# Second mixture of a twelve-stage decoder: its weighted sum on TensorE by diagonals, and earlier first work in two mixtures and a cross-attention

## What is computed

```python
# L2 cross-attention: 16 heads of 64, no softmax
q, k, v = split(layernorm(Q) @ wq), split(layernorm(K) @ wk), split(layernorm(V) @ wv)
out = (l2norm(q) @ l2norm(k).T) @ v            # computed as l2norm(q) @ (l2norm(k).T @ v)
x = Q + out @ wo + bo;  return x + gelu(layernorm(x) @ w1 + b1) @ w2 + b2

# L2 mixture: 8 experts, two per token, each takes at most C = 538 rows
gates = softmax(xf @ Wg.T);  topw, topi = top_k(gates, 2)
within = place_in_expert < C
y = gelu(rows @ W1[e] + b1[e]) @ W2[e] + b2[e]
x = x + sum(topw[:, r] * within[:, r] * y[row of (token, r)] for r in (0, 1))
```

## Time and profile before

| | |
|---|---|
| median of 3 runs | 2631.78 us (2630.09 to 2638.85) |
| the profiled execution | 2638.47 us, span 2637.1 us |
| PE busy, share of the span | 2356.0 us, 89% |
| DVE, ACT, POOL busy | 1207.8, 924.0, 573.2 us |
| mean granted clock of PE | 0.942 of 2.4 GHz |

### The profile page before, as it was taken

One profiled execution on the slowest core, in us unless ns is written; L12 is line 12 of the kernel. 1 busy time (PEld: TensorE's weight loads), 2 busy tenths in 40 slices (PEclk: granted clock), 3 DMA queues, 4 the chain that ended last, 5 costly groups with the idle time before them and its releaser, 6 DMA issues. The chain is left out here.

```text
span 2637.1 us, 34511 instructions
## 1 busy us (share of the span) xinstructions
PE 2356.0 (89%) x13630; PEld 1598.1 (61%) x13630; DVE 1207.8 (46%) x2321; ACT 924.0 (35%) x2500; POOL 573.2 (22%) x587
## 2 busy tenths in 40 slices
PE   6885999998998999786899999689995899989999
PEld 5674777767675665223466656668883478744555
DVE  5644222255787473656234431410006566677442
ACT  2211222242674461554232232022222456434331
POOL 1621222232001011201354420033312100043110
PEclk9977999999999899898899999789997999989999
DMA  5015888840001000200000000322315833210000
GB/s 167 0 33 219 302 303 301 301 157 1 1 2 53 1 2 32 100 1 32 0 1 1 0 1 0 112 73 93 98 45 202 327 148 139 81 36 1 9 9 17
DMA packets 75383, 224.29 MB, mean 85 GB/s; under 512 B 9359, under 2 KB 52757, under 8 KB 65238
## 3 DMA queue, kind: packets, MB, share of 16 engines
q1 hardware_dynamic: 67894, 204.82, 21.4%
q0 software_dynamic: 7328, 17.26, 1.9%
HBM read 178.68 MB, written 45.17 MB: 85 GB/s over the span
## 5 line engine op out<-in xcount | busy, mean ns | idle before, releaser
L221 PE MATMUL psum<-arena 128*128 128x256 f32 (+4 forms) x3716 | 987.5, 423 | 16.1 <-ACT arena L231 3.9
L221 PEld LDWEIGHTS psum<-arena 128*128 128x128 f32 (+1 forms) x3716 | 681.3, 186 | 279.8 <-issue 130.1
L263 POOL TENSOR_SCALAR x_moments<-x_moments 128x4 f32<-128x4 f32 x48 | 12.5, 260 | 879.9 <-DVE x_moments L256 879.5
L1964 DVE TENSOR_REDUCE small<-psum 128x4 f32<-128x1024 f32 (+1 forms) x112 | 137.0, 1223 | 116.4 <-PE psum L1875 65.6
L1234 POOL DMA_INDIRECT l_out<-arena,slot_tables x79 | 78.6, 996 | 412.4 <-ACT arena L1412 234.0
L1937 ACT ACTIVATE arena<-psum,small 128x128 f32<-128x128 f32 (+1 forms) x384 | 148.8, 414 | 51.5 <-DVE small L1964 51.3
L3555 PE MATMUL psum<-arena 128*128 128x512 bf16 x768 | 166.2, 379 | 0.0
L1439 DVE TENSOR_TENSOR arena<-arena,psum 128x352 f32<-128x352 f32 x78 | 40.6, 521 | 253.7 <-ACT arena L1390 253.7
L1975 DVE COPY arena<-psum 128x512 f32<-128x512 f32 x224 | 143.5, 680 | 1.7 <-PE psum L1886 1.5
L1870 PE MATMUL psum<-arena 32*128 32x128 f32 (+1 forms) x1280 | 133.1, 339 | 0.0
L1937 ACT ACTIVATE z<-psum,small 128x128 f32<-128x128 f32 (+1 forms) x256 | 103.8, 426 | 74.8 <-DVE small L1964 74.8
(11 more groups left out here) (360 smaller groups left out, 3480.9 us busy)
## 6 DMA issues: line engine op xcount, KB each, us to landing
arena<-L_ffn_w_in SPq DMA_DIRECT2D x39, 2176.0 KB
arena<-L_ffn_W_in SPq DMA_DIRECT2D x16, 1024.0 KB
positions<-arena SPq DMA_DIRECT2D x16, 1024.0 KB, 5.2
arena<-positions SPq DMA_DIRECT2D x16, 1024.0 KB, 7.8
arena<-l_out SPq DMA_DIRECT2D x16, 512.0 KB, 7.7
positions<-arena SPq DMA_DIRECT2D x16, 512.0 KB, 5.2
arena<-positions SPq DMA_DIRECT2D x16, 512.0 KB, 8.5
arena<-ctx_in SPq DMA_DIRECT2D x2, 2048.0 KB, 10.3
```

What stands on the lines that cost most here:

```text
L221: last = nc.tensor.matmul(out, lhsT, rhs, start=(n == 0), stop=(n == len(pairs) - 1))
L1964: nc.vector.reduce_max(self.minus_top(h), use.bank(u).rearrange("p (h l) -> p h l", l=L), AX_X, negate=True).then_inc(self.topped.up(), 1)
```

## The change

**The second mixture's end.** ACT writes 32 diagonal matrices (the identity scaled by the weight of a choice) behind its last strip. For each group PE waits for both ranks, multiplies each returned tile of rows by the diagonal of its weights and adds the pair in PSUM (8 products of 128 x 256), in banks 0 and 1, 2 and 3, 4 and 5, 0 and 1; DVE adds the bank pair to x in one instruction of 128 x 1024. The next norm's transposes stand between the sums on PE.

```diff
+    def pe_sum(self, g):
+        nc, use, u = self.k.nc, self.uses, self.sum_use[g]
+        bank = use.take(u)
+        for rank in range(2):
+            self.k.pe.wait_ge(self.fetched[g][rank])
+        for j in range(4):
+            i = 4 * g + j
+            mm = products(nc, bank[:, D * j:D * j + D], [(self.diagonals[:, rank, i, :], self.back[:, rank, i, :])
+                                                         for rank in range(2)])
+        mm.then_inc(use.fills(u), 1)
+    def act_diagonals(self):
+        k, act = self.k, self.k.act
+        act.wait_ge(self.router.weighed)
+        act.wait_ge(*self.uses.filled(self.y_use[E - 2][-1]))
+        for rank in range(2):
+            for i in range(TILES):
+                m = k.nc.scalar.activation(self.diagonals[:, rank, i, :], k.ident, ACT.Copy,
+                                           scale=self.router.weights[:, rank, i:i + 1])
+        m.then_inc(self.diagonals_in.up(), 1)
+    def dve_sum(self):
+        k, use = self.k, self.uses
+        for g, u in enumerate(self.sum_use):
+            xs = k.x[:, 4 * g:4 * g + 4, :]
+            k.dve.wait_ge(*use.filled(u))
+            k.nc.vector.tensor_tensor(xs, xs, use.bank(u).rearrange("p (a c) -> p a c", a=4),
+                                      ALU.add).then_inc(use.empties(u), 1)
+            self.next.norm.dve_final(g, use.emptied(u))
...
-        self.finals("pe")
+        pe.wait_ge(self.diagonals_in)
+        for g in range(GROUPS):
+            self.pe_sum(g)
+            self.next.norm.pe_final(g)
...
-        self.dve_combine()
+        self.dve_sum()
```

```diff
+    def pe_turn_first(self, part):
+        use, tiles = self.uses, (range(self.FIRST), range(self.FIRST, self.RT))[part]
+        for a in tiles:
+            self.k.pe.wait_ge(self.first_rows[a])
+        for c in range(DC):
+            u = self.turn_use[0][2 * part + c]
+            self.turned(0, use.take(u), c, tiles).then_inc(use.fills(u), 1)
...
-        self.pe_turn(0)
+        self.pe_turn_first(0)
...
                 for m, u in enumerate(self.h_use[e][half]):
+                    if (e, half, m) == (0, 0, MT // 2):
+                        self.pe_turn_first(1)
```

```diff
+        if self.capacity is not None:
+            dve.wait_ge(self.chosen)
+            dve.step(nc.vector.tensor_tensor(place3, hot3, k.count_up[:, 0:E].unsqueeze(1).to_broadcast([P, 32, E]), ALU.mult))
+            dve.step(nc.vector.reduce_sum(base, place3, AX_X))
         dve.wait_ge(*use.filled(self.use_counts))
...
-        for n, part in enumerate(k.choice_parts):
-            nc.vector.tensor_tensor(self.parts[:, :, tiles * n:tiles * n + tiles], high,
-                                    part.unsqueeze(2).to_broadcast([P, N, tiles]), ALU.mult)
+        nc.vector.tensor_tensor(self.parts[:, :, 0:tiles], high, k.choice_parts[0].unsqueeze(2).to_broadcast([P, N, tiles]),
+                                ALU.mult)
...
     def act(self):
         self.norm.act_zT(GROUPS - 1)
+        self.k.act.wait_ge(self.tiles_in)
+        self.k.nc.scalar.activation(self.parts[:, :, self.tiles:2 * self.tiles], self.tile_hot, ACT.Copy,
+                                    scale=self.k.choice_parts[1][:, 0:1]).then_inc(self.places_in.up(), 1)
```

```diff
+        self.q_use.extend(u.add("sums", 2) for _ in range(2))
+        for g in range(GROUPS):
+            self.ctx_turn.use.append([u.add(engine, 1, 4 + 2 * (g % 2) + c) for c, engine in enumerate(("dve", "act"))])
         context()
-        queries()
...
+        self.norm.pe_zT(0)
+        for mark in self.norm.zT_in(0):
+            pe.wait_ge(*mark)
+        self.pe_queries(0)
         for g in range(GROUPS):
             self.ctx_turn.pe(g, (self.ctx_normed, 4 * g + 4))
...
         self.pe_context(0)
-        self.pe_queries(0)
...
+        self.dve_queries(0)
         self.dve_context(0)
-        self.dve_queries(0)
```

More of the change, by code:

```diff
@@ L1211, in rows_in @@
     def rows_in(self, j):
-        return self.rows_loaded[j % self.rows_ring], self.per * (j // self.rows_ring + 1)
+        return self.rows_loaded[j % self.rows_ring], self.per * (j // self.rows_ring + (0 if j % self.rows_ring < self.apart else 1))
     def y_out(self, j):
@@ L2645, in __init__, with unit @@
         self.renormed = k.counter("z_normed_again", "dve").reserve(GROUPS)
+    def unit(self, what, b, a):
+        return 4 * b + a + (0 if (what == "q") == (b == 0) else 2)
     def pe_rows(self, u, w, srcT, i):
@@ L2941 @@
 class L2Mixture(Mixture):
+    FIRST = 3
     def __init__(self, k):
@@ L2973, in __init__ @@
             self.y_use.append([u.add("dve") for _ in range(RT)])
+        self.sum_use = [u.add("dve", 2, 2 * (g % 3)) for g in range(GROUPS)]
         u.close()
+        self.diagonals = k.arena[:, 4 * SLAB:4 * SLAB + 2 * TILES * P].rearrange("p (r i n) -> p r i n", r=2, n=P)
+        self.diagonals_in = k.counter("weights_on_diagonals", "act").reserve(1)
         self.biases_in = k.loads("expert_biases", 2)
         self.ring = [k.loads(f"expert_weights{n}", E) for n in range(2)]
-        self.rows_shared(RT, E)
+        self.rows_shared(RT, E, 2, 1)
+        self.first_rows = [k.loads(f"first_rows{a}", 1) for a in range(RT)]
     def count(self, a):
@@ L2986, in pe_turn, with turned, empty_turn_first @@
             for c, u in enumerate(self.turn_use[e]):
-                bank = use.take(u)
-                for a in range(self.RT):
-                    n = self.count(a)
-                    tr = nc.tensor.transpose(bank[:, P * a:P * a + n], self.rows[e % 2][0:n, a, P * c:P * c + P],
-                                             k.ident[0:n, 0:n])
-                tr.then_inc(use.fills(u), 1)
+                self.turned(e, use.take(u), c, range(self.RT)).then_inc(use.fills(u), 1)
+    def turned(self, e, bank, c, tiles):
+        for a in tiles:
+            n, at = self.count(a), P * (a - tiles[0])
+            tr = self.k.nc.tensor.transpose(bank[:, at:at + n], self.rows[e % 2][0:n, a, P * c:P * c + P], self.k.ident[0:n, 0:n])
+        return tr
+    def pe_turn_first(self, part):
+        use, tiles = self.uses, (range(self.FIRST), range(self.FIRST, self.RT))[part]
+        for a in tiles:
+            self.k.pe.wait_ge(self.first_rows[a])
+        for c in range(DC):
+            u = self.turn_use[0][2 * part + c]
+            self.turned(0, use.take(u), c, tiles).then_inc(use.fills(u), 1)
+    def empty_turn_first(self, part, engine):
+        k, use = self.k, self.uses
+        span = (slice(0, P * self.FIRST), slice(P * self.FIRST, CAPACITY))[part]
+        for c in range(DC):
+            u = self.turn_use[0][2 * part + c]
+            if use.by(u, engine):
+                (k.dve if engine == "dve" else k.act).wait_ge(*use.filled(u))
+                copied(k, engine, self.rowsT[0][:, c, span], use.bank(u)[:, 0:span.stop - span.start]).then_inc(use.empties(u), 1)
     def empty_turn(self, e, engine):
@@ L3087, in load_rows @@
                 n = self.count(a)
-                self.gather(e, self.rows[e % 2][0:n, a, :], self.RT * e + a, n)
+                self.gather(e, self.rows[e % 2][0:n, a, :], self.RT * e + a, n, None if e else self.first_rows[a])
     def pool(self):
```

78 lines of the change are left out of this document (49 added, 29 removed).

## The result

The kernel after takes 2628.4 us (median of 22 runs, 2620.23 to 2630.54). In 22 runs the kernel before takes 2639.07 us (2630.09 to 2642.76), so the ratio is 0.9965 (95% interval 0.9957 to 0.9974): faster by 10.7 us between the medians, a small change (0.35%) that is clear of the noise. The prediction was 2619.8, in a range of 2612 to 2627: the direction held, the time lies 1.4 us outside the range. The profiled execution after took 2627.89 us (span 2626.6), 10.6 less than that of before.

The account below looks back on a forecast made before the run. PE, busy 89% of the span, bounds the kernel, so gains lie in its waits. Terms -1.4, -2.3, -3.0, -5.5 and +0.2 sum to -12.0 us; from the median 2631.78 that gives 2619.8 us, range 2612 to 2627.

Parts of the forecast that it names:

- Step 1: Both routers: one of two multiplications moves from DVE to ACT, hidden there; 1.4 us gained in the L0 mixture.
- Step 2: Second mixture's router: two instructions move into the wait for counts, 0.9 us; its gathers start 2.3 us earlier with the DVE-to-ACT move.
- Step 3: Second mixture's first rows: PE starts after three gathers and six transposes instead of five and ten; net 3.0 us gained.
- Step 4: Cosine attention: query tiles fill PE's 10.20 us wait, z's transposes come 1.7 us late; 5.5 us gained, bounds 4.4 and 8.2.
- Step 5: Second mixture's tail: sums move from DVE to PE behind loads and low clock; 0.2 us later, bounds -2.9 and +12.
- (c): Rival: low clock through the tail's sums lasts into L3Attention, 10 us more there, +22 in all, 2641.6 us; chance 0.05.
- (b): Rival: tail at low clock through all four sums, +12 in place of +0.2, 2631.6 us, no change; chance 0.04.
- (a): Rival: gains partly lost in L0 router, first rows, cosine and tail; -6.6 in all, 2625.2 us; chance 0.14.
- rows at 0.4: Second mixture's first rows: lower bound, 0.4 us gained if a full tile lands as late as the last one (26 rows).
- the L0 gather tied to the weights: L0 mixture: if its first gather waits for the weights to be in, the router's gain there is 0, not 1.4 us.
- (d): Rival: clock back early in the tail and behind `kv`, -2.0 and -2.5 us more, 2615 us; chance 0.10.

Follow-up runs that it names:

- exp. 7: Kernel after with the routers of both mixtures as in the kernel before; 2631.41 us (12 runs), ratio 0.9974.
- exp. 6: Kernel after with the second mixture's first expert's rows in one piece, PE waiting for all five gathers, as before; 2625.93 us (6 runs), ratio 0.9956.
- exp. 1: Kernel after with the cosine attention as before (queries after the keys, ctx through eight banks); 2635.06 us (12 runs), ratio 0.999.
- exp. 4: Kernel after with 20 unread products on PE in its wait ahead of the tail's sums; 2622.12 us (6 runs), ratio 0.9942.
- exp. 8: Kernel after with earlier ctx copies on DVE, twelve unread products ahead of `kv` and twenty ahead of the tail's sums; 2620.41 us (6 runs), ratio 0.9943.
- exp. 2: Kernel after with the tail's sum of returned rows on DVE as before; 2626.74 us (8 runs), ratio 0.9963.
- exp. 5: Kernel after with twelve unread products on PE in its 6.89 us wait ahead of `kv`; 2627.93 us (7 runs), ratio 0.9966.

## Why the prediction was right or wrong

**The step that failed is the base.** The prediction moved its sum from the profiled execution to the median of three runs: "it lies 6.7 us above the median of 2631.78, and from that the forecast is 2619.8 us". The sum itself, -12.0, had 2626.5 as its like for the profiled execution, and 2627.89 was measured. I took the 6.7 us as an offset of the profiled execution against the others. They were the distance of two groups, and the median of three runs lay in the lower one, because two of the three did; of 22 runs 14 lie in the upper, and the kernel before has a median of 2639.07, 7.3 us higher. Of the 8.6 us by which the forecast missed, 7.3 are this, and 1.3 are the sum (-12.0 for -10.7). With the two series measured beside the experiments 21 of 66 runs lie in the lower group, so three runs have their median there in an estimated quarter of all cases: bad luck, but not rare. The three runs showed it: 2630, 2632 and 2639 aren't a scatter of 0.3% about one value, and the range allowed "1 to 2 us between medians" where 8 was needed. From the median of 22 runs the same sum gives 2627.1.

**The sum**, at the places of the two first profiles:

| step | forecast | measured | in the other profiles |
|---|---|---|---|
| L0 router | -1.4 | -1.5 | -0.7 to -1.4 |
| second router | -2.3 | -2.2 | -2.2 (exp. 7) |
| first rows | -3.0 | -2.7 | -2.4 (exp. 6) |
| cosine, to the next context | -5.5 | -6.0 | -5.3 (exp. 1) |
| from there to the second router's first count | 0 | -2.1 | -2.8 (exp. 1) |
| tail | +0.2 | +0.5 | -0.9 (exp. 1 and 6) |
| L3Attention's start | 0 | +1.6 | 0 (exp. 1, 4, 6, 8), +1.6 in the rest, also behind the old tail (exp. 2) |

**Step 1** was right for DVE's chain, and ACT was hidden: the first gather starts 1.37 us earlier. "Should land 1.4 us earlier" held in two of nine profiles; the mean of the nine is 1.1 (26.99 us from the first count in place of 28.07). By 640 us the kernel after was 3.4 us ahead in its first profile. It stood 0.6 behind at 690, and 0.3 behind at 1227: the stretch at 650 to 680 us ate it. My "passes through to the end" held for the mixture only. **Step 2** was right. **Step 3**'s first bound, that a full tile lands later than the one of 26 rows, was partly true: 2.87 for 2.39 us behind the gather's start. The Trainium skill (DMA: Bandwidth & Descriptors, Anatomy of one DMA — SWDGE (gpsimd) path) gives about 2.0 us and the bytes at 436 KB per us. Counted from the end of that issue (1712.23), the estimate from that page is 1714.5, and PE went on at 1714.10. My row (2.39 us after the start of the issue) gives 1713.6, so the measured time lies half way between the two.

**Step 4**, the largest, was right in its mechanism and nearly in its size: z's transposes 1.7 us later from the stage's start (1.7 forecast), units 5.57 apart, `kv` at 1281.7 (1281.3). `kv` took 3.68 us, inside the bounds of 2.09 and 4.2. What it lacked is what the stage leaves behind: another 2.1 us up to the second router, where a batch that was at low clock before is at full clock (exp. 5). **Step 5** was right in its mechanism: 12.98 for 48 records, where full clock takes 10.60 (exp. 4), is 2.4 us for the clock; I had 2.7. PE began 5.88 us after SP's first load, I had 5.4. The 8.6 us that DVE saves were worth nothing, since the sums stand behind the loads and the clock (exp. 2). The missed part is behind it: L3Attention's first products at low clock, 1.6 us, for which the sum had nothing and rival (c) had 10. They are slow in some profiles and not in others, with the same instructions, and also behind the old tail (exp. 2), so the rewritten sums are not their cause. Whether the rest of the change makes them likelier is not shown. The stretches of the two first profiles add up: 3.4 us ahead at 640 us, 3.7 given back by 1227, then 8.2 won by the second router's first count, 4.9 more by the first strip, 2.1 lost in the tail and L3Attention's start, and 0.2 behind it, which makes the 10.5 us between the spans.

**Rivals.** (b) and (c), the low clock through the tail: it was back within the first sums (0.96 in the window of 1986 to 1988 us), and none of them came. (a), gains partly lost, has a time (2625.2) nearer to the measured one than mine, but only because the base had moved: its change of -6.6 is further from -10.7 than my -12.0. Of its terms, rows at 0.4 fell in experiment 6, and the L0 gather tied to the weights holds for up to half of the 1.4. (d), the clock back early behind `kv` and in the tail, did not come: `kv` took 3.68 us and the first sums 2.4 too long. The rival that I lacked is one that takes nothing from the change: that the base belongs to another group of runs than the median that will be measured.

## What to carry to other kernels

Look at the single times before using their median: when three runs leave a gap of 7 us, forecast from the profiled execution's own time, and let the range reach over the gap. Work moved to an idle PE paid here for the clock which PE had lost in its wait of 10 us (12.98 us in place of 10.60). Twenty products that nobody reads, put into that wait, bought 1.4 to 4.4 us at the place in three lines, while the rewritten sums alone bought nothing. And a gain has to be followed further than its own stage: three edits that won 1.9 to 3.4 us in the cosine stage had each lost 3.2 by the next router. Where a gain of 2 us is to be proved against groups 8 us apart, read the rows at the place from a landmark ahead of it, and say that the total doesn't show it.

## What the runs showed of the hardware that was not expected

The same instructions took 41.7, 43.1 or 47.1 us in one place and 76.2 or 80.3 to 81.4 in another; the windows show another granted clock (0.77 and 0.91 in the first). Gains made ahead of such a place can vanish in it, from run to run as here, or always: a batch of router logits took 1.95 us in six profiles and 3.53 to 3.58 in the seven whose cosine stage ended otherwise. `kv`, 64 products of 64 columns, takes 2.09 us at full clock and 3.68 after PE had stood still for 6.89 us. One execution of the kernel before took 8711 us, though two others took 2631 and 2632. Its granted clock is 0.26 to 0.36 from 2500 us on. Before that it reads 1.00 up to 2200 us, yet PE was as slow: 427 records in the first 500 us, where the first profile of before has 1924. What slowed it stays open.
